# Local attention in two layers: the rows of a tile turned one tile sooner, wide products in front of the second scores, first scores at the end of a turn

## What is computed

```python
h = shift_token(x)                      # second half of the columns comes from the row before
q, k, v = split(h @ wqkv, 3)            # 512 columns each, 8 heads of 64
q = l2norm(q) * q_scale;  k = l2norm(k) * k_scale
q, k = rotary_xpos(q, k)                # rotation with a scale, per position
sim  = einsum('bhwid,bhwjd->bhwij', q * 8.0, look_around(k))
attn = softmax(where(mask, -big, sim))
o = einsum('bhwij,bhwjd->bhwid', attn, look_around(v))
x = x + o @ wo
```

## Time and profile before

| | |
|---|---|
| median of 3 runs | 5537.14 us (5536.8 to 5541.4) |
| the profiled execution: its time | 5540.01 us |
| its span | 5538.4 us |
| granted TensorE clock, mean | 0.942 |
| layer 0 attention, first to last row sums | 1861.7 to 2631.0 us |
| layer 1 attention, the same | 3143.1 to 4090.9 us |
| PE, DVE, ACT, POOL busy over the span | 89%, 75%, 54%, 53% |

### The profile page before, as it was taken

The page is one execution under the profiler, slowest core; times in us unless marked ns, Lnnn a source line. Parts: engine busy times, 40 slices in busy tenths (PEclk is TensorE's granted clock), DMA queues, the critical chain, the costliest instruction groups (busy, mean ns, idle before and its releaser), DMA issues. The chain is left out here.

```text
span 5538.4 us, 79645 instructions
## 1 busy us (share of the span) xinstructions
PE 4910.3 (89%) x26068; PEld 2909.0 (53%) x26068; DVE 4156.5 (75%) x8613; ACT 3011.0 (54%) x6489; POOL 2936.8 (53%) x1617
## 2 busy tenths in 40 slices
PE   6788888888885699999999999999999999998886
PEld 2233233233322477776555566666665555665765
DVE  3999999999999699999433477777763337995259
ACT  4877886887776477777211255555541114453232
POOL 4999999999999465655111244444431110002732
PEclk9898888889887799999999999999999999999997
DMA  5666566566555223223112111111111133444768
GB/s 134 152 157 148 142 160 159 139 150 160 147 132 129 77 85 91 86 88 103 46 57 63 45 35 35 37 38 36 46 52 47 57 117 129 159 141 126 196 147 177
DMA packets 493021, 585.39 MB, mean 106 GB/s; under 512 B 59446, under 2 KB 372548, under 8 KB 488516
## 3 DMA queue, kind: packets, MB, share of 16 engines
q1 hardware_dynamic: 461412, 554.19, 36.7%
q0 software_dynamic: 29184, 18.78, 2.3%
q10 hardware_dynamic: 2016, 7.34, 0.4%
HBM read 416.67 MB, written 180.37 MB: 108 GB/s over the span
## 5 line engine op out<-in xcount | busy, mean ns | idle before, releaser
L684 POOL TENSOR_TENSOR db<-durep,brep 128x2048 f32<-128x2048 f32 x256 | 1160.5, 4533 | 101.4 <-DVE p_h L589 87.6
L536 ACT ACTIVATE p_h<-dlrep,am 128x512 f32<-128x512 f32 x1024 | 700.4, 690 | 159.8 <-DVE hh L600 134.4
L589 DVE TENSOR_TENSOR_SCAN p_h<-p_h,hlast,db 128x512 f32<-128x512 f32 x576 | 718.3, 1278 | 21.8 <-ACT hlast L525 17.7
L1302 POOL TENSOR_TENSOR rot_cos<-rot_cos,rot_sin 128x1024 f32<-128x1024 f32 x128 | 302.2, 2361 | 536.1 <-DVE rot_sin L1223 536.1
L1298 POOL TENSOR_TENSOR rn<-n,mhalf 128x16 f32<-128x16 f32 x128 | 374.7, 2928 | 266.7 <-DVE n L1233 266.6
L600 DVE TENSOR_TENSOR hh<-p_h,crep 128x512 f32<-128x512 f32 x768 | 516.1, 672 | 0.0
L352 PE MATMUL p_acc<-hh,fold 128*32 128x512 f32 x2048 | 310.1, 681 | 207.4 <-DVE hh L600 206.1
L1665 POOL TENSOR_TENSOR grstd<-grstd,mhalf 128x4 f32<-128x4 f32 x32 | 32.6, 1019 | 729.1 <-DVE grstd L1582 728.9
L980 PE MATMUL p_s<-qkT 64*128 64x128 f32 x4096 | 300.3, 286 | 75.6 <-DVE nb L1188 74.4
L1567 ACT ACTIVATE gg<-p_s,b 128x512 f32<-128x512 f32 x160 | 110.0, 687 | 448.5 <-PE p_o L1510 265.8
L1091 ACT ACTIVATE probB<-probB,nb 128x256 f32<-128x256 f32 x512 | 254.4, 499 | 164.9 <-DVE nb L1188 164.9
(11 more groups left out here) (290 smaller groups left out, 11730.1 us busy)
## 6 DMA issues: line engine op xcount, KB each, us to landing
dlrep<-delta_rows SPq DMA_DIRECT2D x256, 256.0 KB
durep<-drive_rows SPq DMA_DIRECT2D x256, 256.0 KB
ew<-in_L_ffn_w SPq DMA_DIRECT2D x192, 176.0 KB
first_queries_keys<-qs SPq DMA_DIRECT2D x128, 256.0 KB, 2.4
qk<-first_queries_keys SPq DMA_DIRECT2D x64, 512.0 KB, 3.8
brep<-bc_rows SPq DMA_DIRECT2D x64, 256.0 KB
crep<-bc_rows SPq DMA_DIRECT2D x64, 256.0 KB
delta_rows<-dl SPq DMA_DIRECT2D x64, 256.0 KB
```

The source lines that it names most:

```text
L536: act.activation(p_h[:, (i % BANKS) * CH:(i % BANKS + 1) * CH], dlrep[use % 2][:, j], ACT.Exp, scale=am[:, q, j, g:g + 1]).then_inc(s_ex, 1)
L589: dve.tensor_tensor_scan(out=state, data0=bank, data1=db[s % 2][:, j], initial=0.0 if first else hlast[:, i % TILES:i % TILES + 1], op0=AL ...
L684: pool.tensor_tensor(out=db[s % 2][:], in0=durep[use % 2][:], in1=brep[c % 2][:, g:g + 1, :].to_broadcast([P, 4, CH]), op=ALU.mult).then_i ...
L1302: pool.tensor_tensor(out=rc[:], in0=rc[:], in1=rsn[:], op=ALU.add).then_inc(s_rot, 1)
```

## The change

All calls stay, with the same operands and sizes; their order changes on PE, ACT and DVE. POOL's and SyncE's programs are the same. On PE S0 of tile t + 1 now stands at the end of turn t, in front of T1(t) (layer 0) or in front of I and T1(t) (layer 1). I is done a turn sooner. In front of S1(t) stands V (layer 0) or the first part of QK (layer 1), and W1(t - 1) follows S1(t). On DVE C1(t - 1) stands behind M0(t) in both layers, and rotate is cut up: the two sine products come first (in layer 0 with the residual between them), the cosine product last. On ACT, in layer 0, bring and squares stand ahead of O.

```diff
@@ tensor: the loop over t
-            if now:
-                scores(t, 0)
-            if f < NT:
+            if t < 0:
                 turn_in(f)
-            if t >= 1:
-                weighted_values(t - 1, 1)
-            if now:
-                scores(t, 1)
             if made:
                 if f < NT:
                     values(f)
                 if now:
-                    turn_prob(t, 0)
+                    scores(t, 1)
                 if t >= 1:
-                    project(t - 1, 0)
-                    project(t - 1, 1)
-                ...
-                    turn_qk(t + 1)
+                    weighted_values(t - 1, 1)
             else:
-                ...
                 if f < NT:
                     queries_keys(f, 0)
                 if now:
-                    turn_prob(t, 0)
+                    scores(t, 1)
+                if t >= 1:
+                    weighted_values(t - 1, 1)
                 if f < NT:
                     queries_keys(f, 1)
-                ...
+            if now:
+                turn_prob(t, 0)
+            if t >= 1:
+                project(t - 1, 0)
+                project(t - 1, 1)
+            ...
+            if 0 <= t + 1 < NT:
+                turn_qk(t + 1)
+            if f < NT and not made:
+                values(f)
+            if t >= -1 and f + 1 < NT and made:
+                turn_in(f + 1)
             if now:
                 weighted_values(t, 0)
+            if 0 <= t + 1 < NT:
+                scores(t + 1, 0)
+            if t >= -1 and f + 1 < NT and not made:
+                turn_in(f + 1)
+            if now:
                 turn_prob(t, 1)
@@ scalar
             if now:
-                exps(t, 0, (0, 1))
-            ...
+                exps(t, 0, range(4))
             if made:
                 if f < NT:
+                    bring(f)
                     squares(f)
-                if now:
-                    exps(t, 1, (0, 1))
-                    turn_prob(t, 0)
-                    exps(t, 1, (2, 3))
-            else:
+                if t >= 1:
+                    turn_out(t - 1)
                 if now:
                     exps(t, 1, (0, 1))
                     turn_prob(t, 0)
                     exps(t, 1, (2, 3))
                 if f < NT:
+                    values(f)
+                if 0 <= t + 1 < NT:
+                    turn_qk(t + 1)
+            else:
+                if t >= 1:
+                    turn_out(t - 1)
+                if now:
+                    exps(t, 1, range(4))
+                    turn_prob(t, 0)
+                ...
+            if t >= -1 and f + 1 < NT:
+                turn_in(f + 1)
@@ vector
             if made:
                 if now:
                     maxima(t, 0)
+                if t >= 1 and now:
+                    turn_prob(t - 1, 1)
                 if 0 <= t + 1 < NT:
                     square_sums(t + 1)
                 if now:
                     normalise(t, 0)
                     maxima(t, 1)
                     turn_prob(t, 0)
+                if f < NT:
+                    rotate_half(f, 0)
                 if t >= 1:
                     residual(t - 1)
+                if f < NT:
+                    rotate_half(f, 1)
                 if now:
                     normalise(t, 1)
                 ...
                 if f < NT:
                     rotate(f)
-                if now:
-                    turn_prob(t, 1)
```

More of the change, by code:

```diff
@@ L1058, in tensor @@
                 if now:
-                    turn_prob(t, 0)
+                    scores(t, 1)
+                if t >= 1:
+                    weighted_values(t - 1, 1)
                 if f < NT:
                     queries_keys(f, 1)
[L1062 to L1065, removed]
+            if now:
[3 more added lines that the diff above has]
+                project(t - 1, 1)
+            if t == NT - 1:
+                next(then)
+            if 0 <= t + 1 < NT:
[4 more added lines that the diff above has]
+                turn_in(f + 1)
             if now:
                 weighted_values(t, 0)
+            if 0 <= t + 1 < NT:
[3 more added lines that the diff above has]
+            if now:
                 turn_prob(t, 1)
@@ L1133, in scalar @@
                 turn_prob(t - 1, 1)
-            if f < NT and made:
-                bring(f)
-            if f < NT:
+            if t < 0:
                 turn_in(f)
             if now:
-                exps(t, 0, (0, 1))
[L1140 to L1145, removed]
+                exps(t, 0, range(4))
             if made:
                 if f < NT:
+                    bring(f)
                     squares(f)
-                if now:
-                    exps(t, 1, (0, 1))
-                    turn_prob(t, 0)
-                    exps(t, 1, (2, 3))
-            else:
+                if t >= 1:
+                    turn_out(t - 1)
                 if now:
@@ L1206, in turn_prob, with table, rotate_half @@
             dve.tensor_copy(tf[:, INNER:2 * INNER], p_t[:, INNER:2 * INNER]).then_inc(s_pe[half], 1)
-        def rotate(f):
[L1209 to L1214, removed]
+        def table(f, s, a, n):
+            tk = tab[f % 2][:].rearrange("p (a s) c -> p a s c", a=2)
+            return tk[:, :, s, a:a + n].unsqueeze(2).to_broadcast([P, 2, H, n])
+        def rotate_half(f, half):
+            if half == 0:
+                dve.wait_ge(s_tab, n0 + f + 1)
+                if f > 0:
+                    dve.wait_ge(s_rot, n0 + f)
+                dve.wait_ge(s_sq, n0 + f + 1)
+            a, b = half * HK, HK - half * HK
+            dve.tensor_tensor(out=rs4[:, :, :, a:a + HK], in0=qk4[:, :, :, b:b + HK], in1=table(f, 1, a, HK), op=ALU.mult)
+        def rotate(f):
             if f > 0:
                 dve.wait_ge(s_qkT, n0 + f)
[L1217 to L1224, removed]
+            dve.tensor_tensor(out=rc4, in0=qk4, in1=table(f, 0, 0, DK), op=ALU.mult).then_inc(s_rs, 1)
         def square_sums(f):
@@ L1260, in vector @@
                     next(then)
+                    turn_prob(t, 1)
                 if f < NT:
                     rotate(f)
+            else:
                 if now:
-                    turn_prob(t, 1)
-            else:
+                    maxima(t, 0)
                 if t >= 1:
                     turn_prob(t - 1, 1)
-                if now:
-                    maxima(t, 0)
                 if 0 <= t + 1 < NT:
@@ L1279, in vector @@
                     normalise(t, 1)
+                if t >= 1:
+                    residual(t - 1)
                 if t == NT - 1:
```

19 lines of the change are left out of this document (5 added, 14 removed).

## The result

| | before | after |
|---|---|---|
| median | 5538.71 us (4 runs, 5536.8 to 5541.4) | 5463.57 us (4 runs, 5460.3 to 5469.5) |
| ratio | | 0.9865, 95% interval 0.9852 to 0.9877 |
| the profiled execution: time, span | 5540.01, 5538.4 | 5466.42, 5464.8 |
| layer 0, first to last row sums | 769.4 us | 747.2 us |
| layer 1, the same | 947.8 us | 898.7 us |

The kernel became 75 us faster by the medians, 73.6 by the two profiled spans. Of these 22.2 lie in layer 0, 49.1 in layer 1 and 2.3 around them.

The account below looks back on a forecast made before the run. PE's wait before S1 was taken to bound layer 1 with PE's own work; in layer 0 the PE-DVE loop, POOL's nearly tied. 19 + 27 = 46 us off 5540.0 gives 5494, less 2.9: 5491 us; range 5464 to 5520.

Parts of the forecast that it names:

- The wait in front of S1: PE's wait for DVE's nb, 0.53 us a turn in layer 0, 0.56 in layer 1, goes in both.
- Layer 0: Turn falls from 12.11 to 11.80 us, set by POOL's loop: 0.31 a turn, 19 us, bounds 6 to 27.
- the near ties: In layer 0, four paths end between 11.4 and 11.8 us; the longest, POOL's 11.80, was taken.
- the walk: Step-by-step timing of one layer 0 turn in the new order, M0's start at 0, from profile rows.
- Layer 1: The turn becomes PE's own work: 0.45 us a turn less, 27 us over 61 turns, bounds 21 to 37.
- 0.12 for Q: In layer 1, Q costs 1.00 us instead of 0.88, as it now stands behind J and before V.
- the ends of layer 1: First and last turns of a layer: nothing, give or take one wait of half a us a layer.
- The bound for the gain a turn, 0.60: Upper bound of layer 1's gain a turn, in us, allowing T1 up to 0.16 less; the lower was 0.35.
- Rival 1: Weight loads hidden behind wide products in layer 1: S1, W1, T1 cheaper, Q stays 0.88; 61 us there, 5457; chance 0.11.
- Rivals 2 to 4: Layer 0 gives nothing, 5510, 0.16; both layers' gains eaten, 5530, 0.08; slower by ACT's queue in layer 0, 5557, 0.09.
- rival 4: ACT's queue in layer 0, loop from J to J, makes a turn of 12.9 us: slower, 5557; chance 0.09.

Follow-up runs that it names:

- old_qk_before_S1: The kernel before with one move in layer 1, the first part of QK in front of S1 instead of behind J: 5513.0 us (0.9956).
- v_copy_earlier: The changed kernel with ACT in layer 0 copying V in front of the second half of E1 instead of behind it: 5457.3 us (0.9854).
- sums_before_C1: The changed kernel with DVE in layer 0 making the sums in front of C1 again: 5468.9 us (0.9871).
- rows_behind_T1: The changed kernel with I behind T1 instead of in front of it in layer 1: 5516.4 us (0.9961).
- W1_behind_qk: The changed kernel with W1 behind the second part of QK instead of in front of it in layer 1: 5518.9 us (0.9963).
- tighter: The changed kernel with, in layer 0, sums before C1, I before T0, V's copy before bring and squares behind O: 5540.9 us (1.0002).

## Why the prediction was right and where it failed

**The wait in front of S1: right.** It is gone in both layers, and `old_qk_before_S1` shows that it held layer 1.

**Layer 0: right in size, by luck, with the wrong loop in front.** 11.80 was forecast, 11.78 measured; Q came 8.05 us behind M0, PE waited 0.42 in front of T0 (0.35 forecast), J started 6.06 behind M0 (6.02). But of the near ties the one that binds is ACT's copy of V, not POOL: the walk had it end at 8.95 with 0.1 to spare, and it ended at 8.92 with a hand-over of 0.14. The number held by luck. The sum priced Q at 1.00 and I at 0.36, where they take 0.90 and 0.31 when nothing holds them, so POOL's own loop is 11.64 and not 11.80, which is the turn of `v_copy_earlier`; ACT's loop, which the walk took for covered, happens to be 11.78. Whoever had acted on it, by relieving POOL, would have got nothing, as `sums_before_C1` did. The layer gave 22 us where 19 were forecast.

**Layer 1: the failed step.** "Its sum isn't simply 15.08 - 0.55, since a group costs by its neighbours" was the right question, and the answer was wrong in sign. The forecast added 0.12 for Q and took nothing for T1, J, I and W1. J took 1.84 in the old order (the row shown with `old_qk_before_S1`), and the rows of T1 to W1 there are:

```profile
3513.21 1.09 PE L997 MATMUL p_t<-ident,probB 128*128 128x128 f32 x8
3514.24 1.16 PE L980 MATMUL p_s<-qkT 64*128 64x128 f32 x16
3515.33 0.44 PE L930 MATMUL p_v<-ident,hx 128*128 128x128 f32 x2
3515.70 1.09 PE L1011 MATMUL p_o<-probT,v 128*64 128x128 f32 x16
```

From the old order to the new, over the steady turns: Q the same, T1 0.15, J 0.10, I 0.09 and W1 0.07 less, the two parts of QK 0.10 more each. That is 0.22 less on top of the wait's 0.56, 0.78 in all, where 0.45 was forecast: over 61 turns 20 of the 28 us by which the profiled time fell short of the forecast. The other 8 are layer 0's 3, some 2 at the ends of layer 1, and 2 around the layers, put at nothing. The 0.12 for Q were read from layer 0, where Q costs 1.00; there W0 stands behind it. J in front, which the forecast blamed, costs it nothing: Q takes 0.87 behind J in the new order of layer 1. The bound for the gain a turn, 0.60, was too tight as well: it let T1 vary and held the rest at single rows, though J, I and the neighbours of S and W were just as unmeasured in the new order.

What sets these costs are the crossings. The old turn has three groups in front of S or W (V, I, T1: 0.30), J and T1 behind one (0.15), and W1 in front of a wait (0.07). The new one has two in front (V, QK: 0.20) and one behind (QK: 0.10). The difference is the 0.22. The rule was made from the rows and then gave 14.45 for an order that had not been run, which came out at 14.45 once a new wait had been taken out of it. The Trainium skill's page "TensorEngine Tiling (Array Packing)", section "Key Properties", says that changing the tiling mode drains TensorE. The trace agrees in kind, with 0.05 to 0.10 us for a crossing, and with weights that are never loaded ahead across one. That a drain is what holds the loads back, and why transposes behind S or W pay half, no run here shows.

**Rival 1** was right for T1 (0.15 less, it had 0.16) and for Q, and wrong for S1 and W1: they cost 1.09 and 1.02 in the new order, not 0.92 and 0.86. S1 stands behind a wide product there, and its weights are not loaded ahead for that. The rest of the saving is in the groups beside them.

**Rivals 2 to 4** didn't come. ACT's queue, which rival 4 feared, is the one that binds, by its branch to I rather than to J, but at 11.78 and not above 12.

## What to carry to other kernels

Where several engines close loops of nearly one length, relieve them together: one edit alone reads as worthless though it is half of a good pair. When groups of products that use half the array and groups that use all of it alternate, put the half-array groups side by side, and price an order by counting the crossings, not by the durations of the old neighbours. Before moving a step, list who waits for its copy and who is queued behind it on the copying engine: three of the twelve kernels here lost 50 us or more to a new wait, one for the copy itself (`rows_behind_T1`) and two by ACT's queue (`W1_behind_qk`, `tighter`).

## What the hardware showed that I had not expected

The same part of QK (L940, 128x512) occupies PE for 1.71 us between transposes, 1.82 with a half-array group on one side and 1.92 with one on both. Eight transposes take 0.88, 0.93 behind a half-array group and 1.03 between two. In the profile the extra time shows as no idle row; only the distance of starts tells it, and the row of the weight load, which isn't ahead of the product. Short waits hide in the same way: in `sums_before_C1` Q takes 1.18 because I waits for ACT, and I's row has no idle time. So a long step is not yet a crossing; look first at when the operand of the next group was ready. The hand-over from ACT to PE was 0.14 us in front of I, where I had used less than 0.1.
